# Values copied into PSUM by ScalarE before the scans' products, late scans two slots later, and split second products in the eight slots behind each unit's scans

## The reference, cut to what matters

```python
x = hidden_states                                   # (2, 1024, 128)
x = x + 0.5 * ffn(layernorm(x))
x = x + attention(layernorm(x))
x = x + 0.5 * ffn(layernorm(x))

def ffn(x):                                         # 8 experts, two are chosen per token
    gates = top-2 of softmax(x @ router_w.T), normalised
    h = relu(x @ w1[e].T + b1[e]);  y[e] = h @ w2[e].T + b2[e]     # w1: 512x128
    return sum over e of gates[e] * y[e]

def attention(x):                                   # 4 heads, 16 keys and 32 values each
    r, w, k, v, g = projections of x + (shifted x - x) * mu
    step t:  kv = k_t[:, None] * v_t[None, :]
             o_t = q_t . (S + u * kv);  S = exp(-exp(w_t)) * S + kv
    return (groupnorm(o) * silu(g)) @ W_o.T
```

## Time and profile before

| | |
|---|---|
| median of 3 runs | 519.8 us (519.72 to 519.86) |
| the profiled execution's own time | 519.58 us |
| its span, first to last instruction | 517.7 us |
| PE busy | 491.5 us (95%) |
| DVE busy | 342.4 us (66%) |
| ACT busy | 277.2 us (54%) |
| POOL busy | 249.1 us (48%) |
| mean granted TensorE clock | 0.992 |

### The profile page before, as it was taken

How to read it: one execution, slowest core, us unless ns; L and a number is a source line. 1 busy time by engine, 2 the same in 40 slices (tenths; PEclk the granted TensorE clock), 3 DMA queues, 4 the chain that set the end, 5 groups by cost and what they waited for, 6 DMA issues and landing times.

```text
span 517.7 us, 5924 instructions
## 1 busy us (share of the span) xinstructions
PE 491.5 (95%) x1822; PEld 294.1 (57%) x1822; DVE 342.4 (66%) x647; ACT 277.2 (54%) x465; POOL 249.1 (48%) x245
## 2 busy tenths in 40 slices
PE   6999999999998999799999988999997999999996
PEld 2666666465455546355654644564563555677774
DVE  2663277759954594997476899835769982576443
ACT  3666577653344664243556633336752334577873
POOL 1143341549955161987506278842617884213222
PEclk9999999999999999899999999999999899999999
DMA  7291111065310008540003544110154421003100
GB/s 230 56 363 45 41 42 41 3 203 164 123 41 1 0 1 225 163 142 1 0 3 122 142 145 149 54 62 3 38 143 148 138 82 41 1 0 123 62 0 20
DMA packets 20574, 43.51 MB, mean 84 GB/s; under 512 B 3776, under 2 KB 3904, under 8 KB 20544
## 3 DMA queue, kind: packets, MB, share of 16 engines
q1 hardware_dynamic: 14208, 31.61, 19.0%
q10 hardware_dynamic: 6336, 11.54, 6.9%
HBM read 39.86 MB, written 3.28 MB: 83 GB/s over the span
## 4 chain that ended last, share of the span: by engine, by line
PE 61%; issue 14%; DVE 11%; POOL 9%; ACT 3%; POOLq 0%; ACTq 0%; DVEq 0%
PE Y L318 21%; PE U L297 9%; PE U L299 8%; PE U L298 7%; POOL xT L821 3%; PE A L387 3%; POOL qs L842 2%; DVE hid_lo L692 2%; PE Y L313 2%; PE Y L314 2%; PE Y L315 2%; DVE pool_a L746 2%; ACT xnt L486 1%; DVE gy L701 1%; DVE pool_a L729 1%
## 5 line engine op out<-in xcount | busy, mean ns | idle before, releaser
L514 ACT ACTIVATE hid<-U,small 128x512 f32<-128x512 f32 x188 | 128.7, 689 | 164.7 <-PE U L299 151.6
L318 PE MATMUL Y<-hid,w 128*128 128x512 f32 x376 | 193.6, 597 | 0.0
L297 PE MATMUL U<-xhi,w1lo 128*128 128x512 f32 x256 | 168.3, 658 | 3.8 <-ACT hid L514 2.6
L821 POOL TENSOR_TENSOR xT<-xT,gy 128x512 f32<-128x512 f32 x64 | 87.7, 1370 | 159.9 <-DVE gy L701 159.9
L299 PE MATMUL U<-xhi,w1hi 128*128 128x512 f32 x256 | 101.6, 397 | 0.0
L298 PE MATMUL U<-xlo,w1hi 128*128 128x512 f32 x256 | 101.2, 395 | 0.0
L842 POOL TENSOR_TENSOR qs<-q,pool_a 128x512 f32<-128x512 f32 x64 | 83.3, 1302 | 14.7 <-DVE pool_a L729 14.7
L297 PEld LDWEIGHTS U<-xhi,w1lo 128*128 128x128 f32 x256 | 48.6, 190 | 72.0 <-issue 54.1
L318 PEld LDWEIGHTS Y<-hid,w 128*128 128x128 f32 x376 | 71.5, 190 | 16.5
L692 DVE TENSOR_TENSOR hid_lo<-hid,hid_hi 128x512 fp32r<-128x512 f32 x68 | 54.0, 799 | 32.0 <-ACT hid_hi L512 31.7
L298 PEld LDWEIGHTS U<-xlo,w1hi 128*128 128x128 f32 x256 | 48.9, 191 | 38.0 <-issue 36.2
(11 more groups left out here) (119 smaller groups left out, 474.8 us busy)
## 6 DMA issues: line engine op xcount, KB each, us to landing
G<-gate_dram SPq DMA_DIRECT2D x32, 512.0 KB, 3.9
vb<-v_dram ACTq DMA_DIRECT2D x44, 256.0 KB, 3.2
vb<-v_dram SPq DMA_DIRECT2D x20, 256.0 KB, 4.5
pool_a<-wexp_dram SPq DMA_DIRECT2D x8, 256.0 KB, 7.0
w<-wexp_dram SPq DMA_DIRECT2D x8, 256.0 KB, 7.1
v_dram<-v SPq DMA_DIRECT2D x8, 256.0 KB, 2.3
xT<-xT_dram SPq DMA_DIRECT2D x4, 256.0 KB, 7.7
out_dram<-xT SPq DMA_DIRECT2D x4, 256.0 KB, 3.1
```

The source lines that it names most:

```text
L297: mm(dst, w1lo[:, e, f, :], xhi[:, k % NB, :], start=True, stop=False)
L318: mm(dst, w2[:, g % E, f, :], hid[:, n % HS, :], start=first, stop=final).then_inc(down, 1)
L514: act.activation(hid[:, n % HS, :], U[n % 2][:, :], ACT.Relu, bias=bias).then_inc(h_f, 1)
L821: pool.tensor_tensor(xT[:, h, b, :], xT[:, h, b, :], gy[:, g % 2, :], ALU.add).then_inc(acc, 1)
```

## The change

ACT copies each row of values from `vb` into the PSUM bank one slot ahead of the scan (`show`), and DVE's product reads that bank instead of `vb` and writes back into it. `vb` is free for the next load when the copy is done (semaphore `vp` in place of `kv_r`), and `fetch` now follows `show`. For units 2 and 3 the steps from `T_HOLD` = 15 on come two slots later (`PAUSE`). The stretch without split second products ends at step 40 instead of 48, which makes 24 more of the 256 slots split, 92 after 68: 77, 78, 80, 81, 82, 84, then 120, 121, 122, 124, 125, 126, then 136, 137, then 164, 165, 166, 168, then 178, 180, 181, then 208, 209, 210. `PREP` of blocks 3, 6 and 7 and `UNIT[3]` move, and SP issues `values` ahead of the gates of the same slot.

```diff
--- before.py
+++ after.py
@@ -21,8 +21,9 @@
 RH = NS * NH
 UNITS = 2 * NB
 EPS = 1e-5
-PREP = [None, 6, 34, 80, 119, 129, 170, 212]
-UNIT = [37, 79, 121, 163]
+PREP = [None, 6, 34, 77, 119, 129, 172, 216]
+UNIT = [37, 79, 121, 165]
+PAUSE = (0, 0, 2, 2)
 
 LAG = 3
 EQ = 2
@@ -34,7 +35,7 @@
 T_DEV, T_NRM, T_CHN, T_LO = 1, 2, 4, 5
 T_LG, T_EXP, T_RT = 6, 7, 8
 T_XM, T_Z, T_MUS, T_PR, T_SC = 5, 7, 9, 12, 18
-SC = 20
+T_HOLD, SC = T_PR + 3, 20
 T_PO = T_SC + SC + 2
 T_VAR, T_OUT = T_PO + 2, T_PO + 8
 MIX = (1, 0, 2, 3, 4)
@@ -52,6 +53,16 @@
 W_ALL = W_GB + 1
 
 
+def step_of(i, n):
+
+    t = n - UNIT[i]
+    return t if t < T_HOLD else max(t - PAUSE[i], T_HOLD)
+
+
+def slot_of(i, t):
+    return UNIT[i] + t + (PAUSE[i] if t > T_HOLD else 0)
+
+
 def gates_slot(k, c):
 
     if k == 0 and c < GS // EQ:
@@ -74,8 +85,8 @@
 
 
 LN_FFN, LN_ATT = layernorms()
-ROUTED = [1 + sum(PREP[k] + T_LG < UNIT[i] + T_SC for k in range(1, BLOCKS)) for i in range(UNITS)]
-SCANNED = [0] + [sum(UNIT[i] + T_SC < PREP[k] for i in range(UNITS)) for k in range(1, BLOCKS)]
+ROUTED = [1 + sum(PREP[k] + T_LG < slot_of(i, T_SC) for k in range(1, BLOCKS)) for i in range(UNITS)]
+SCANNED = [0] + [sum(slot_of(i, T_SC) < PREP[k] for i in range(UNITS)) for k in range(1, BLOCKS)]
 
 
 def home(k):
@@ -90,7 +101,7 @@
 
 def in_parts(n):
 
-    scans = any(start + T_SC - 3 <= n < start + T_OUT for start in UNIT)
+    scans = any(slot_of(i, T_SC) - 3 <= n < slot_of(i, T_PO) for i in range(UNITS))
     return n >= SLOTS and n % FC < FP and not scans
 
 
@@ -191,7 +202,7 @@
         xa_zero, xa_prev, xm_r, z_p, z_r, mus, mterm, u_r = (sem(n) for n in ("xa_zero", "xa_prev", "xm_r", "z_p", "z_r", "mus", "mterm", "u_r"))
         pr, aw_r, q_r, k_r, quk_r, bet, bet_c, bv_r = (sem(n) for n in ("proj", "aw_r", "q_r", "k_r", "quk_r", "beta", "beta_c", "bv_r"))
         v_r, sg_t, sg_r, wb_r, e_r, dec_r = (sem(n) for n in ("v_r", "sg_t", "sg_r", "wb_r", "e_r", "dec_r"))
-        kv_r, st_r, qs_r, red, o_r, seed, s_zero = (sem(n) for n in ("kv_r", "st_r", "qs_r", "red", "o_r", "seed", "s_zero"))
+        vp, kv_r, st_r, qs_r, red, o_r, seed, s_zero = (sem(n) for n in ("vp", "kv_r", "st_r", "qs_r", "red", "o_r", "seed", "s_zero"))
         cen, sq_r, var_p, ysc_r, yoff_r, yo_r, yp, x_att = (sem(n) for n in ("cen", "sq_r", "var_p", "ysc_r", "yoff_r", "yo_r", "yp", "x_att"))
 
         block = ctx.enter_context(nc.Block())
@@ -235,7 +246,7 @@
                 for m in range(VS):
                     n = i * VG + m
                     if n >= VS:
-                        sp.wait_ge(kv_r, n - VS + 1)
+                        sp.wait_ge(vp, n - VS + 1)
                     sp.dma_start(vb[:, n % VS, :], value_rows(v_dram[i], m)).then_inc(v_in[n % VS], 16)
 
             def rows_out(k):
@@ -261,6 +272,9 @@
             sp.dma_start(w(0, W_RT), small_in[:, 0:W_RT]).then_inc(small_l, 16)
             rows_in(3)
             for n in range(ALL):
+                for i in range(UNITS):
+                    if n == UNIT[i] + T_PR + 1:
+                        values(i)
                 for k in range(1, BLOCKS):
                     if n == PREP[k] + T_RT + 3:
                         gates_to_rows(k)
@@ -268,9 +282,6 @@
                     for c in range(NQ):
                         if n == gates_slot(k, c):
                             gates_in(k, c)
-                for i in range(UNITS):
-                    if n == UNIT[i] + T_PR + 1:
-                        values(i)
                 for k in (4, 5):
                     if n == (k + 1) * SLOTS + 8:
                         rows_out(k)
@@ -468,7 +479,7 @@
                 for k in range(1, BLOCKS):
                     prepare(k, n - PREP[k])
                 for i in range(UNITS):
-                    attend(i, n - UNIT[i])
+                    attend(i, step_of(i, n))
             for last in range(LAG):
                 ffn_down(ALL - LAG + last)
 
@@ -528,16 +539,31 @@
 
             def fetch(i, m):
                 n = i * VG + m
-                act.wait_ge(kv_r, n - VS + 1)
+                act.wait_ge(vp, n - VS + 1)
                 act.dma_start(vb[:, n % VS, :], value_rows(v_dram[i], m)).then_inc(v_in[n % VS], 16)
+
+            def show(i, m):
+                n = i * VG + m
+                if m == 0:
+                    act.wait_ge(bet_c, i + 1)
+                if m == 1:
+                    act.wait_ge(bv_r, i + 1)
+                if m == 2:
+                    act.wait_ge(sg_r, i + 1)
+                if m >= 3:
+                    act.wait_ge(st_r, n - 2)
+                act.wait_ge(v_in[n % VS], 16 * (n // VS + 1))
+                act.activation(A[STATE_BANK[m % 3]][:, :], vb[:, n % VS, :], ACT.Copy).then_inc(vp, 1)
 
             def attend(i, t):
                 h, b = home(i)
                 if t == T_NRM:
                     normalise(LN_ATT[i], A[0])
-                m = scan_at(t - 1)
-                if m is not None and m + VS < VG:
-                    fetch(i, m + VS)
+                m = scan_at(t + 1)
+                if m is not None:
+                    show(i, m)
+                    if m >= 1 and m + VS - 1 < VG:
+                        fetch(i, m + VS - 1)
                 if t == T_CHN:
                     act.wait_ge(ln_T, LN_ATT[i] + 1)
                     if h == 1:
@@ -717,8 +743,8 @@
             def scan(i, m):
                 n, (h, b) = i * VG + m, home(i)
                 bank = A[STATE_BANK[m % 3]][:, :]
-                dve.wait_ge(v_in[n % VS], 16 * (n // VS + 1))
-                dve.tensor_tensor(bank, vb[:, n % VS, :], kk[:, :], ALU.mult).then_inc(kv_r, 1)
+                dve.wait_ge(vp, n + 1)
+                dve.tensor_tensor(bank, bank, kk[:, :], ALU.mult).then_inc(kv_r, 1)
                 if n >= SS:
                     dve.wait_ge(qs_r, n - SS + 1)
                 if m == 0:
```

## The result

The changed kernel takes **512.68 us** (median of 4 runs, 512.02 to 515.3) against 519.83 us for the kernel before (4 runs beside it, 519.72 to 520.3). The ratio is 0.987, with a 95% interval of 0.9835 to 0.9905: faster by 7.15 us, where 7.4 were forecast (512.4). The profiled execution took 512.65 us, its span 510.8, against a span of 517.7 before. Two executions of the kernel before that ran beside the first four experiments (617.64 and 528.27 us) were in the chip's slower state and are left out of medians and ratios.

The account below looks back on a forecast made before the run. PE's matmul chain was taken to bound the kernel, with DVE almost equal in the scans. -11.2 - 1.4 + 3.3 + 1.9 + 0.0 = -7.4 from 519.6 gives 512.2, plus 0.2: 512.4 us, range 505.0 to 517.0.

Parts of the forecast that it names:

- The scans: Four scan stretches: gains of 0.6, 5.0, 2.1 and 3.5 us in units 0 to 3, together -11.2 us.
- Products and copies: In the scans: DVE's product takes 0.69 us, freeing 10 us of DVE; 64 copies on ACT cost nothing.
- the rival of a slow product: The 64 products: reading and writing one PSUM bank is slow, making the kernel slower, about 547 at 1.38 us; chance 0.08.
- Unit 1's values: Unit 1's scans: first value comes 4.7 us earlier, before the first scan slot, so 5.0 us of excess go.
- 32.76 + 3.60 = 36.4 us of work: Each scan stretch: PE's work in 21 slots with three reduces; anything longer counted as excess.
- Unit 2: Unit 2's scans: start two slots later, lateness falls from 3.8 to 2.2 us, 1.3 stay as waiting; gain 2.1 us.
- the lateness falls from 3.8 to 3.8 - 3.1 + 1.5 = 2.2: Scans of units 2 and 3: two slots later saves 3.1 us, two new `hid_lo` add 1.5; unit 3 gains 3.5.
- Behind unit 1: After unit 1's layer norm: DVE waits for a split slot's `hid_hi` and does three more `hid_lo`, +3.4 us.
- may give back a little; I take +3.3: After unit 1: later waits return a little of the +3.4 us delay, leaving +3.3.
- Behind unit 2: After unit 2's layer norm: added pairs and `hid_lo` end L780 at 359.7, 1.9 us after PE came; +1.9 us.
- +1.2 - 1.2, together 0: Behind unit 0: PE's product moves from 173.94 to 175.1, +1.2 us; PE's 1.2 us wait for five `u` goes.
- The eight splits expected to save 0.17 us each: Slots 136, 137, 178, 180, 181 and 208 to 210: PE keeps the split's saving there, -1.4 us.

Follow-up runs that it names:

- the first four experiments: Four kernels: the changed one without the eight slots' splits (504.39 us) or without copies (519.75); the kernel before with only those splits (527.8) or only copies (516.99).
- twice_copied: Changed kernel with the no-split stretch ending at step 48 again and each of the 64 copies made twice: 503.72 us, ratio 0.9688.
- copies_only: Kernel before with only the copies into PSUM, the loads behind them and the product in its bank, nothing moved: 516.99 us, ratio 0.9936.
- prep_early: Kernel before with only block 3's preparation three slots earlier and the values' loads ahead of the gates in SP's queue: 512.32 us, ratio 0.9855.
- no_eight: Changed kernel with the no-split stretch ending at step 48 again, leaving out 19 of the 24 further splits: 504.39 us, ratio 0.9686.
- split_125: Changed kernel with the no-split stretch ending at step 48 again, but the second products of slots 125 and 126 split: 506.95 us, ratio 0.9736.

## Why the forecast came out, step by step

The scans were forecast at -11.2 us and gave -14.7; everything else at +3.8 and gave +7.8. That 512.4 came so close is luck.

**Products and copies: right.** 0.69 us was taken for the product and 0.680 came; of the 64 before, 18 took 0.98 to 1.48 us, and none does now (0.70 at most), so the rival of a slow product is out. The Trainium skill ("VectorE: DVE Perf Modes", the section on the TRN2 errata) gives 120 fixed cycles from PSUM and 58 from SBUF, by the forecast's estimate 65 ns more for the product. That is not borne out: 680 ns here against the 0.67 us of the undisturbed one from SBUF. That copies are hidden was argued from ACT's 14 us; `twice_copied` shows it. What they are worth alone is 3.3 us (`copies_only`).

**Unit 1's values: right in cause, 0.7 too small.** 5.67 against 5.0. `prep_early`, without any copy, gets the same 35.70 us, so the queue and the preparation do it; but it pays 1.3 us of them back in the next slot, which the copies save and the forecast did not see. The step that was mis-sized is the floor, "32.76 + 3.60 = 36.4 us of work": a stretch that nothing holds takes 35.7 in units 1 and 3. The forecast also had the first value there before the first scan slot (199.1 for 200.1) and DVE not idle; DVE waited 2.10 us, the product ran 0.7 us into the slot (201.11) and PE waited for nothing: the first `reduce` stands only in the seventh slot.

**Unit 2: right.** The first product was forecast 2.2 us into its slot and came 298.88 - 296.65 = 2.2 us into it; 1.3 us of waiting were to stay, and PE stands 37.08 - 35.77 = 1.31.

**Unit 3: the step "the lateness falls from 3.8 to 3.8 - 3.1 + 1.5 = 2.2" failed.** It fell to 389.44 - 388.93 = 0.5, and no waiting was left. The two `hid_lo` were added as if both stood in an unbroken row, as they do in unit 2, where DVE takes 9.28 us from `o` (L782) to the first product, 7.64 before. Ahead of unit 3's `o` DVE sits idle for 2.71 us, until ACT has `quk`:

```profile
381.67 0.69 DVE L782 TENSOR_TENSOR o<-A,quk 128x512 f32<-128x512 f32 x1 [2.71 <-ACT quk L592]
```

A `hid_lo` in front of such a gap costs nothing. Behind it stands one more than before, 0.6 us, but a short instruction of the routing that had been a long one is short again:

```profile
385.03 1.05 DVE L672 TENSOR_TENSOR rt<-rt,rs 128x32 f32<-128x32 f32 x1
```

```profile
386.03 0.19 DVE L698 TENSOR_TENSOR rt<-rt,rs 128x32 f32<-128x32 f32 x1
```

The first is before, the second with the change, the same instruction. So from `o` to the first product it is 7.77 us, 8.04 before. The forecast treated both units alike; why the long one went is not shown.

**Behind unit 1: the chain was right, what follows it was not.** `xT` was forecast 3.4 us later and is 3.44 later. The "may give back a little; I take +3.3" is the failed step: instead of giving back, the wait was followed by matmuls at the lower clock level, 1.3 us. **Behind unit 2** 2.06 for 1.9: PE gets `xT` 25.7 us into the stretch, and the forecast's 359.7 was 25.8 us into it.

**Behind unit 0: "+1.2 - 1.2, together 0" failed in both halves.** The moved preparation is worth 3.3 there, not 1.2 (`prep_early`, `no_eight`): beside the one wait that was read the earlier trace rows PE had waited there 0.7 us for ACT's `xnt` and 0.7 for `aw`, and in `no_eight` it waits for nothing; and the splits cost 3.6, not 1.2, because they were priced against the place where PE stood before the move (173.94), and by then the move alone would have had PE there earlier (172.78 in `no_eight`, which starts the stretch 0.8 us later). The product that was forecast at 175.1 came at 175.68; the layer norm ended 0.5 us earlier, not 0.9. One term was netted against another before either was sized, and the result looked calm.

**The eight splits expected to save 0.17 us each** are seen behind unit 3 alone: its stretch holds five split second products more than before, for -0.8 us (0.17 each); those of 208 to 210 are new, and those of 212 and 213 were split before too, but further on. Among the rest, 0.7 us is the start of the first slot (12.68 against 12.03 us), which lies anywhere from 11.9 to 13.1 us in the kernels here and is no effect of the change. 0.6 is in the tail's 16 slots, where block 7's gates are written four slots later and DVE waits 3.8 us for them:

```profile
DVE gy L727 <- DMA G<-gate_dram: 3.8, 1, 3.8
```

That wait was not in the forecast. But the place of the gates alone does not cost it: the eight other kernels with block 7 at 216 wait 2.3 to 2.9 us at the same instruction, and their 16 slots take 22.9 us, as before. Why it is 3.8 in this one is open. The range held because the terms erred in both directions; of the two halves neither was within 3 us.

## What to carry to other kernels

Split a change before judging it: here two edits that look like housekeeping (a preparation three slots earlier, a small load ahead of a large one in a queue) give 7.4 us, two more (copies and late scans) give another 8, and the part that removes work from the busiest engine costs 8. A split, or any work added in front of a way that the busiest engine waits for, costs its full length there even if it shortens that engine's own work, and where an unrelated group of small instructions stands on the same way, moving the awaited instruction past them is worth more than trimming it. Price each edit against the kernel with the other edits in it, and look for gaps at each place, since the same two instructions cost 1.6 us in one unit and nothing on balance in the next. An edit that seems to give little alone (the copies, 3.3 us) can be what the next ones need: with the other lateness gone, PE meets the engines that it had been hiding.

## What the runs showed of the hardware that was not expected

- A `tensor_tensor` of 128x512 that reads and writes the same PSUM bank takes 680 ns in the mean, as one with both operands in SBUF does when nothing disturbs it (0.67 us), and the long ones (18 of 64, up to 1.48 us, each begun while POOL ran `qs<-q,pool_a`) are gone. POOL gains too: that product of its own takes 1188 ns for 1302 before (1187 in `copies_only`, where nothing else changed), and its busy time in a scan stretch falls from 32 to 27 us, though nothing was changed on it.
- ACT's copy from SBUF into PSUM takes 594 ns, against 622 for its activation within SBUF.
- The granted clock fell to its lower level behind a PE wait of 3.47 us in the changed kernel (matmul pairs at 1.50 and 1.92 us for 1.10 and 1.05) and not behind one of 3.48 us in `split_125`. What decides between the two is open; it made some 1 to 2 us of difference in a stretch, as large as several of the terms that were compared.
